# Two graph layers with residual norms on one core: the second layer's products in another order, and another root in the tail

## What is computed

```
def _layernorm(x, axis=-1, eps=1e-05):
    m = jnp.mean(x, axis=axis, keepdims=True)
    v = jnp.var(x, axis=axis, keepdims=True)
    return (x - m) / jnp.sqrt(v + eps)
...
        sim = jnp.tanh(adj * simlar)
        filt = sim * (adj > 0).astype(sim.dtype)
        vals, idx = jax.lax.top_k(filt, T)
...
        h2 = jnp.tanh(h @ W_proj + b_proj)
        feat = jax.nn.relu(new_adj @ (h2 @ W_gcn) + b_gcn)
...
        pos = jnp.matmul((node_adj > 0).astype(feats.dtype), feats)
        neg = jnp.matmul((node_adj < 0).astype(feats.dtype), feats)
        node_support = jnp.concatenate([pos, neg], axis=1)
        node_output = jnp.matmul(node_support, node_weight)
        node_output = node_output + node_bias * jnp.diagonal(edge_adj)[:, None]
        edge_support = jnp.matmul(edge_adj, feats)
        edge_output = jnp.matmul(edge_support, edge_weight)
        edge_output = edge_output + edge_bias * jnp.diagonal(node_adj)[:, None]
        return node_output + edge_output
    x = _layernorm(x + _L0_gnn_ref(x, adj, adj, ...), axis=-1)
    x = _layernorm(x + _L1_gnn_ref(x, adj, adj, ...), axis=-1)
```

## Time and profile before

| | us |
|---|---|
| median of 3 runs (621.15 to 621.41) | 621.28 |
| the profiled execution, its own time | 622.29 |
| its span, first to last instruction | 620.5 |
| PE busy | 603.0 |
| DVE busy | 475.7 |
| ACT busy | 415.7 |
| first product with `adj` in the first layer (L913) / in the second (L922) | 30.6 / 254 |
| copy of the last sums starts | 610.16 |
| last rows scaled | 616.13 |

### The profile page before, as it was taken

One profiled execution on the slowest core, in us unless ns is written; L12 is line 12 of the kernel. 1 busy time (PEld: TensorE's weight loads), 2 busy tenths in 40 slices (PEclk: granted clock), 3 DMA queues, 4 the chain that ended last, 5 costly groups with the idle time before them and its releaser, 6 DMA issues.

```text
span 620.5 us, 5693 instructions
## 1 busy us (share of the span) xinstructions
PE 603.0 (97%) x1966; PEld 342.3 (55%) x1966; DVE 475.7 (77%) x703; ACT 415.7 (67%) x293; POOL 186.7 (30%) x79
## 2 busy tenths in 40 slices
PE   7799999999999999999999999999999999999994
PEld 5544444444444444555655655655655656558993
DVE  2676979788887979986697696796786886877735
ACT  2378686868687686548784883983883874856850
POOL 0387697978879697000000000000000000000000
PEclk9899999999999999999999999999999999999998
DMA  8999999999999980048889398486595684883000
GB/s 235 336 347 347 330 282 315 270 328 287 324 281 298 315 197 0 1 135 229 219 250 252 97 246 232 127 243 188 154 250 154 186 248 125 230 232 96 2 18 18
DMA packets 141181, 130.65 MB, mean 211 GB/s; under 512 B 9443, under 2 KB 141158, under 8 KB 141158
## 3 DMA queue, kind: packets, MB, share of 16 engines
q1 hardware_dynamic: 74982, 66.22, 38.4%
q10 hardware_dynamic: 66176, 64.17, 37.2%
HBM read 128.27 MB, written 2.10 MB: 210 GB/s over the span
## 4 chain that ended last, share of the span: by engine, by line
PE 94%; DMA 2%; ACTq 2%; ACT 1%; DVE 1%; issue 0%
PE acc L913 35%; PE acc L922 33%; PE stage L924 10%; PE stage L923 10%; PE stage L922 2%; DMA x_rows<-in_x_dram 2%; PE to_rows L932 1%; PE to_rows L933 1%; ACTq L457 1%; ACTq L460 1%; PE to_rows L898 1%; PE stage L881 1%; ACT a_cols L520 0%; PE to_cols L887 0%; ACT a_cols L515 0%
## 5 line engine op out<-in xcount | busy, mean ns | idle before, releaser
L581 DVE STREAM_TRANSPOSE a_cols<-a_rows 128x2048 f32<-128x2048 f32 x128 | 294.6, 2306 | 90.8 <-PE stage L924 55.1
L922 PE MATMUL acc<-a_cols,x_rows 128*128 128x512 f32 (+1 forms) x512 | 248.1, 566 | 0.0
L913 PE MATMUL acc<-a_cols,rhs 128*128 128x512 f32 x512 | 221.4, 593 | 1.3 <-ACT a_cols L520 1.3
L923 PE MATMUL stage<-masks,x_hi 128*128 128x512 f32 (+1 forms) x288 | 208.5, 724 | 0.0
L354 POOL TENSOR_TENSOR a_cols<-a_cols 128x1536 f32<-128x1536 f32 x64 | 175.2, 2746 | 63.5 <-DVE a_cols L581 62.9
L913 PEld LDWEIGHTS acc<-a_cols,rhs 128*128 128x128 f32 x512 | 96.6, 190 | 120.4 <-issue 120.4
L520 ACT ACTIVATE a_cols<-a_cols 128x2048 f32<-128x2048 f32 x64 | 122.3, 1912 | 50.6 <-POOL a_cols L354 49.4
L536 ACT ACTIVATE a_rows<-a_rows 128x4096 f32<-128x4096 f32 x32 | 116.0, 3624 | 26.4 <-DVE a_cols L581 13.3
L539 ACT ACTIVATE a_rows<-a_rows 128x4096 f32<-128x4096 f32 x32 | 115.9, 3623 | 1.0
L924 PE MATMUL stage<-masks,x_lo 128*128 128x512 f32 (+1 forms) x288 | 106.7, 370 | 0.0
L922 PEld LDWEIGHTS acc<-a_cols,x_rows 128*128 128x128 f32 x512 | 94.0, 189 | 20.1 <-issue 0.5
(11 more groups left out here) (84 smaller groups left out, 234.1 us busy)
## 6 DMA issues: line engine op xcount, KB each, us to landing
a_rows<-in_adj_dram SPq DMA_DIRECT2D x120, 512.0 KB, 8.9
a_rows<-in_adj_dram ACTq DMA_DIRECT2D x120, 512.0 KB, 10.0
out_dram<-n_rows SPq DMA_DIRECT2D x28, 64.0 KB, 8.4
x_rows<-in_x_dram SPq DMA_DIRECT2D x6, 128.0 KB, 4.2
x_rows<-in_x_dram ACTq DMA_DIRECT2D x6, 128.0 KB, 5.5
x_rows<-in_x_dram SPq DMA_DIRECT2D x4, 64.0 KB, 2.3
x_rows<-in_x_dram ACTq DMA_DIRECT2D x4, 64.0 KB, 2.7
diag<-in_adj_dram SPq DMA_DIRECT2D x16, 1.0 KB
```

Of the source, the lines that this page charges most:

```text
L581: nc.vector.transpose(half_out(hs), half_in(s, h % HALVES)).then_inc(turned[layer], 1)
L913: last = nc.tensor.matmul(acc[parity][:], rhs[:, b, :], a_cols[:, h % HSLOTS, k, :], start=(b == 0), stop=(b == BLOCKS - 1))
L922: nc.tensor.matmul(sums, x_rows[:, b, :], cols, start=(b == 0), stop=(b == BLOCKS - 1))
L923: nc.tensor.matmul(sums_m, x1_hi[:, b, :], mask, start=(b == 0), stop=False)
```

## The change

Four things are changed, all in the second layer.

1. In each half, PE issues the fp32 products of its four blocks first (`with_adj`), then the masked ones (`with_masks`). In the last chunk's first five halves: fp32 of part 0, fp32 of part 1, masked of part 0, masked of part 1. In the first chunk the four transposes of layer one's last rows stand between the two groups of the first half.
2. In the last three halves the fp32 products of a part come for all its halves before the masked ones, and have a signal of their own: `last_summed` stands behind the fp32 products and lets ACT copy them, a new `last_masked` behind the masked ones lets DVE copy those.
3. PE adds the residual: an fp32 product of the identity with `y_rows` opens the accumulation of a part's rows (`part_y`), the two z products follow, then the two masked-sum products. DVE's addition in `last_norm` is gone, and the statistics and the scaling read PSUM. Ahead of the second `part_y`, PE waits until the root of part 0 is finished, since that uses scratch columns in the same bank.
4. The root of the two parts: ACT takes the square root of variance plus eps (`eps` is a new column that POOL fills at the start), DVE takes the reciprocal and makes one Newton step. ACT takes one Sqrt of a constant ahead of its first copy.

```diff
+            nc.gpsimd.memset(eps[:], EPS).then_inc(consts, 1)
...
             each_chunk(layer1)
+            act.wait_ge(consts, 3)
+            nc.scalar.activation(root_v[:, 0:1], ones[:, 0:1], ACT.Sqrt)
             for part, (at, tiles) in enumerate(PARTS):
                 act.wait_ge(last_summed, part + 1)
                 nc.scalar.copy(by_tile(z_t[:])[:, :, at:at + tiles, :],
                                last_acc[part][:, 0:tiles * P].rearrange("f (q m i) -> f q m i", q=QUARTERS, i=SQ))\
                     .then_inc(sums_kept, 1)
+                act.wait_ge(ln_step, LN_STEPS * (2 * CHUNKS - 1 + part) + 2)
+                nc.scalar.activation(root_v[:, 0:tiles], mean_var[:, 0:tiles, 1], ACT.Sqrt, bias=eps[:, 0:1])\
+                    .then_inc(root_taken, 1)
...
+                def short_root():
...
+                    waited(ln_step, base + 2)
+                    nc.vector.tensor_scalar(v, mean_var[:, 0:tiles, 1], EPS, None, ALU.add).then_inc(ln_step, 1)
+                    waited(root_taken, root_of + 1)
+                    nc.vector.reciprocal(r, root_v[:, 0:tiles]).then_inc(ln_step, 1)
+                    waited(ln_step, base + 4)
+                    nc.vector.scalar_tensor_tensor(out=m, in0=r, scalar=-0.5, in1=r, op0=ALU.mult, op1=ALU.mult)\
+                        .then_inc(ln_step, 1)
+                    waited(ln_step, base + 5)
+                    nc.vector.tensor_tensor(t, v, m, ALU.mult).then_inc(ln_step, 1)
+                    waited(ln_step, base + 6)
+                    nc.vector.scalar_tensor_tensor(out=r, in0=t, scalar=1.5, in1=r, op0=ALU.add, op1=ALU.mult)\
+                        .then_inc(ln_step, LN_STEPS - 6)
...
             def last_sums_m(part):
                 at, tiles = PARTS[part]
-                dve.wait_ge(last_summed, part + 1)
+                dve.wait_ge(last_masked, part + 1)
...
             def last_norm(part):
                 at, tiles = PARTS[part]
-                y = y_rows[:, at:at + tiles, :]
                 dve.wait_ge(rows_ready, 2 * CHUNKS + part)
-                dve.wait_ge(y_step, CHUNKS)
-                nc.vector.tensor_tensor(y, y, last_rows[part], ALU.add).then_inc(y_ready, 1)
-                dve.wait_ge(y_ready, 2 * CHUNKS + part)
...
-                for step in norm(LN_STEPS * (2 * CHUNKS - 1 + part), lambda k: y[:, k, :],
-                                 lambda k: n_rows[:, LAST[2], at + k, :], tiles, dve.wait_ge):
+                for step in norm(LN_STEPS * (2 * CHUNKS - 1 + part), lambda k: last_rows[part][:, k, :],
+                                 lambda k: n_rows[:, LAST[2], at + k, :], tiles, dve.wait_ge, part):
                     step()
...
+            pe.wait_ge(consts, 3)
...
-            def products(sums, sums_m, b, cols, mask):
-                nc.tensor.matmul(sums, x_rows[:, b, :], cols, start=(b == 0), stop=(b == BLOCKS - 1))
-                nc.tensor.matmul(sums_m, x1_hi[:, b, :], mask, start=(b == 0), stop=False)
-                return nc.tensor.matmul(sums_m, x1_lo[:, b, :], mask, start=False, stop=(b == BLOCKS - 1))
-
-            def block_products(parity, h, k):
-                return products(acc[parity][:], acc_m[parity][:], h * HB + k, a_cols[:, h % HSLOTS, k, :],
-                                masks[:, h % HSLOTS, k, :])
+            def all_rows(cols):
+                return cols
+            def with_adj(sums, h, rows):
+                for k in range(HB):
+                    b = h * HB + k
+                    last = nc.tensor.matmul(sums, x_rows[:, b, :], rows(a_cols[:, h % HSLOTS, k, :]), start=(b == 0),
+                                            stop=(b == BLOCKS - 1))
+                return last
+            def with_masks(sums_m, h, rows):
+                for k in range(HB):
+                    b = h * HB + k
+                    mask = rows(masks[:, h % HSLOTS, k, :])
+                    nc.tensor.matmul(sums_m, x1_hi[:, b, :], mask, start=(b == 0), stop=False)
+                    last = nc.tensor.matmul(sums_m, x1_lo[:, b, :], mask, start=False, stop=(b == BLOCKS - 1))
+                return last
...
-                    for k in range(HB):
-                        last = block_products(0, h, k)
-                        if h == 0 and k == 0:
-                            turn_to_rows(LAST)
-                    last.then_inc(half_used[1], 1)
+                    with_adj(acc[0][:], h, all_rows)
+                    if h == 0:
+                        turn_to_rows(LAST)
+                    with_masks(acc_m[0][:], h, all_rows).then_inc(half_used[1], 1)
...
-                    for k in range(HB):
-                        last = block_products(parity, h, k)
-                    last.then_inc(half_used[1], 1)
+                    with_adj(acc[parity][:], h, all_rows)
+                    with_masks(acc_m[parity][:], h, all_rows).then_inc(half_used[1], 1)
                     if h == 0:
                         chunk_rows(before)
...
+                def part_y(part):
+                    at, tiles = PARTS[part]
+                    nc.tensor.matmul(last_rows[part].rearrange("p t f -> p (t f)"), ident[:],
+                                     y_rows[:, at:at + tiles, :].rearrange("p t f -> p (t f)"), start=True, stop=False)
                 def part_rows(part):
                     at, tiles = PARTS[part]
                     pe.wait_ge(sums_kept, CHUNKS + part)
+                    for k in range(tiles):
+                        nc.tensor.matmul(last_rows[part][:, k, :], blk(z_t, at + k), w_pne[:, 2, :], start=False,
+                                         stop=False)
                     pe.wait_ge(sums_m_kept, CHUNKS + part)
-                    if part == 0:
-                        pe.wait_ge(y_ready, 2 * CHUNKS - 1)
-                    weigh(last_rows[part], at, tiles)
+                    for k in range(tiles):
+                        last = nc.tensor.matmul(last_rows[part][:, k, :], blk(sm_t, at + k), w_pne[:, 0, :],
+                                                start=False, stop=(k == tiles - 1))
+                    last.then_inc(rows_ready, 1)
...
                 for h in range(apart):
                     pe.wait_ge(masked, LAST[0] * HPC + h + 1)
-                    half_products(h, 0)
-                    half_products(h, 1).then_inc(half_used[1], 1)
+                    part_adj(h, 0)
+                    part_adj(h, 1)
+                    part_masks(h, 0)
+                    part_masks(h, 1).then_inc(half_used[1], 1)
                     if h == 0:
                         chunk_rows(before)
                 for h in range(apart, HPC):
+                    pe.wait_ge(turned[1], LAST[0] * HPC + h + 1)
+                    last = part_adj(h, 0)
+                last.then_inc(last_summed, 1)
+                for h in range(apart, HPC):
                     pe.wait_ge(masked, LAST[0] * HPC + h + 1)
-                    last = half_products(h, 0)
-                last.then_inc(last_summed, 1)
+                    last = part_masks(h, 0)
+                last.then_inc(last_masked, 1)
                 pe.wait_ge(stats_step, 1)
...
-                half_products(apart, 1)
+                part_adj(apart, 1)
+                part_masks(apart, 1)
...
+                pe.wait_ge(y_ready, 2 * CHUNKS - 1)
+                pe.wait_ge(y_step, CHUNKS)
+                part_y(0)
                 part_rows(0)
                 for h in range(apart + 1, HPC):
-                    last = half_products(h, 1)
+                    last = part_adj(h, 1)
                 last.then_inc(last_summed, 1)
+                pe.wait_ge(ln_step, LN_STEPS * 2 * CHUNKS)
+                part_y(1)
+                for h in range(apart + 1, HPC):
+                    last = part_masks(h, 1)
+                last.then_inc(last_masked, 1)
                 part_rows(1)
```

More of the change, by code:

```diff
@@ L108, in build @@
         rstd = sb("rstd", [P, TILES])
+        root_v = sb("root_v", [P, TILES])
+        eps = sb("eps", [P, 1])
         y2 = sb("y2", [P, TILES])
@@ L240, in build @@
         last_summed = sem("last_summed")
+        last_masked = sem("last_masked")
+        root_taken = sem("root_taken")
         y_ready = sem("y_ready")
@@ L635, in scaled @@
                     ins.then_inc(normed, 1)
-                return stats, root, scaled
+                return stats, root if root_of is None else short_root, scaled
             def norm0(chunk, part):
```

18 lines of the change are left out of this document (10 added, 8 removed).

## The result

The changed kernel takes 618.22 us (median of 5 runs, 618.01 to 618.95) against 621.41 for the kernel before beside it; the ratio is 0.9945 with a 95% interval of 0.9934 to 0.9956, that is 3.4 us less, 2.7 to 4.1. Forecast were 1.6 us less and at most 3.0. The direction was right, the size half of the truth, and the time lies just outside the range. A second measurement gave a ratio of 0.9933 (0.9919 to 0.9947).

The account below looks back on a forecast made before the run. The prediction took PE's products to bound the second layer's middle, then DVE's chain of dependent short instructions the tail. From the median: 621.28 - 1.2 (tail) - 0.4 (grouping) = 619.7 us; 8-in-10 range 618.3 to 621.3.

Parts of the forecast that it names:

- Grouping: Second layer: 448 switches between fp32 and masked products fall away at 1 ns each, 0.4 us gained, bounds 0 and 1.8.
- The prediction's own sign of being wrong: Wrong if a masked product inside a run differs from 234 or 118 ns by more than 4; two other signs.
- Rival A: Second layer: the masked products' excess is a switch price growing with width; 7.7 us gained, 612.4 us; chance 0.08.
- Grouping at half width: Last chunk, 256 columns: 112 of the 448 lost switches, at 1 ns gained each.
- Rival B: Half-width masked runs: weight loads of 190 ns set the pace; 8.1 us lost, 627.8 us; chance 0.07.
- The tail: Kernel's end on PE, DVE and ACT: 0.86 - 0.44 - 0.45 - 1.17 = -1.20 us.
- Identity products: Tail on PE: two new fp32 pairs of 256 columns, 0.43 us each, both on PE's path, +0.86 us.
- End: Last masked product's load to last rows scaled: two fewer weighings -0.44, no DVE residual addition -0.45, shorter root -1.17.
- from the eps row to the scaling: Tail's root: 0.05 + 0.29 (Sqrt) + 0.05 + 0.80 (four DVE instructions) = 1.19 us instead of 2.36.
- The cover ahead of the second identity product: Tail on PE: part 0's root ends at 607.2, PE arrives at 608.6, so the wait is covered by 1.4 us.
- ACT's table load: Loading the Sqrt table, 1.28 us behind ACT's last accumulator read, is over by 599.1 and costs nothing.
- the moved transposes: First chunk: four transposes start at 257.4, done by 258; DVE takes them at 258.92, hidden with 0.9 us to spare.

Follow-up runs that it names:

- half_alternate: Changed kernel with the old fp32, masked, masked order in the last chunk's first five halves: from that chunk's first fp32 load to its last masked load 47.14 us, not 47.30.
- the probe: Changed kernel plus product runs nobody reads behind its last weighing, other engines soon resting: 24 masked products of 256 columns took 120 ns each.
- old_root: Changed kernel with the old root (seed, three Newton steps on DVE) in the tail: from the last masked product's load to the last rows scaled 5.57 us, 1.18 more.

## Why the prediction was right and wrong

**Grouping: the step that failed.** The step drew a line through two widths, 19.5 ns of excess at 512 columns and 10.5 at 256, and concluded that the excess goes with the columns and stays in a run. It took the excess of a product that has an fp32 neighbour for one quantity. It is two: 13.3 ns fixed for each masked product, whatever the width, and a price of starting a run, which is 7 ns a product in pairs at 512 columns and slightly below nothing at 256. Their sums over the columns at 2.4 GHz, 20.3 and 11.6 ns, lie by chance nearly on a line through zero. The whole grouping was taken as 0.4 us gained, with 1.8 as its bound; it measured 2.54 at full width less 0.24 at half width, 2.3. The prediction's own sign of being wrong appeared: a masked product inside a run differs from 234 ns by 7. The bound was too narrow for the same reason: it used the line's intercept. Rival A named the missing view ("a pure run was never seen"), and gave it 8% and a price of 7.7 us, since it let the whole excess vanish; in a settled run a third of it vanished. The Trainium skill's figure for warm matmuls (TensorE: Matmul & The Clock Gate, Wait — 56ns, not 53.3ns?), 216 ns at N = 512, is not reached by these products: 226.7 is their settled pace. Had I put a partial A between the forecast and the full A, the range would have held.

**Grouping at half width** was to gain as well; it costs. Last was +1.09 where the two identity products are 0.85, so 0.24 us for 64 blocks; half_alternate shows 0.17 of it for 40.

**Rival B** is refuted: half-width runs of 16 and 24 keep 120 ns a product (in the probe a run of 24), and loads follow one another at 112.

**The tail** held part by part. Identity products +0.86 forecast, 0.85 measured by taking them away. End -2.06 forecast (-0.44, -0.45, -1.17), -2.01 measured. Sqrt took 0.29, and from the eps row to the scaling are 612.25 - 611.06 = 1.19 us, as worked out. A reciprocal of two columns costs what its neighbours do, 0.17. Two small terms were missing and nearly cancel: the scaling from PSUM takes 0.13 longer, and the masked weighings begin 0.04 us behind the copy where the weighings began 0.14 behind it. The cover ahead of the second identity product was shorter than forecast, as its weight load waits and not the product: that load starts at 606.27 and part 0's root ends at 605.20, so 1.1 us where 1.4 were forecast; old_root shows that it matters. ACT's table load, the moved transposes and the memset cost nothing, as said.

**The numbers.** -1.2 - 0.4 was forecast. Measured were 0.85 - 2.01 = -1.16 for the tail and -2.54 + 0.24 = -2.3 for the grouping. The error is the grouping's alone.

## What to carry to other kernels

Where the pace of a stream of equal instructions is in doubt, measure it in the neighbourhood that the change makes, not in the old one: a price that was read from pairs said nothing about runs, and a fit through two sizes can be straight by chance when two causes overlap. Single-pass products of 512 columns among two-pass fp32 ones gained 2% here from runs of eight behind eight (1.829 us for eight instead of 1.869), and 3% where a run had settled; runs of four gained next to nothing. And ask of work moved to the bounding engine what it takes off the path: the residual on PE cost 0.85 us and took 0.33 away.

## What the runs showed of the hardware

- A masked (fp32r) product in a settled run costs its columns at 2.4 GHz and 13.3 ns: 226.7, 173.3 and 120.0 ns for 512, 384 and 256 columns, at a granted clock of 1.00; at 128 columns it takes 111.6. An fp32 instruction of two passes costs 2.5 ns over its columns (429.2 and, at half width, 215.8).
- How such a run of 512 columns starts depends on what PE did before it. Where runs of twelve follow one another, three products are 5 ns dearer behind 8 or 16 fp32 instructions, and about ten differ behind 2 or 4, 35 ns more in the sum of eleven. But the long start also appears behind 8 (270 and 275 us in the changed kernel) and behind 16. The short start was the same with another bank ahead, another bank at each product, one streamed slot, and the other engines at rest. Why is open.
- DVE's scaling of two tiles takes 0.73 us from PSUM and 0.60 from SBUF, while the statistics take 0.49 from either.
